# Weights split in place, identity products ahead of the first convolution, the rates moved behind the ring fills, and a last step without a recurrent state

## The chip, the cores and the metric

The kernel runs on one core of one Trainium2 chip. The metric is the device time of one execution in microseconds (us), as the median of several runs. The profile is of one execution; its span goes from the first to the last instruction.

## The reference, cut to what matters

Two layers are added onto `x` (128 batch rows, 128 time steps, 512 features), one after the other:

```python
# layer 0, a gated scan steered by cond (128 x 512)
conv = conv_b + causal convolution of x with cond as its 128 taps, per feature
proj = conv @ Wp + bp                      # 512 -> 128
B_t, C_t = softplus(proj[:64]), tanh(proj[64:])
u = x @ Ws + bs                            # 512 -> 64
dt = softplus(dt_log); decay = 1 - dt * softplus(A_log)
state = decay * state + dt * B_t * u ;  y = C_t * state
x = x + y @ Wo + bo
# layer 1, a recurrence over time, h0 = cond
h = tanh(h @ Wh + x[:, t] @ Wx + b)        # 512 -> 512
x[:, t] = x[:, t] + h
```

`dt` and `decay` (the "rates") come from two small vectors. `dt` is multiplied into the rows of `Wo`.

## The kernel before, in words

**Number format.** Most products are made with float32 operands split into a high part `*_hi` (type fp32r) and a rest `*_lo`. A weight is split by GpSimd (POOL): a cast to `*_hi`, then a subtraction into `*_lo`. The small weight Ws is split the same way into the two halves of `ws_hl`.

**Stage 1, four times (chunks c = 0 to 3 of 128 features).** `convolution(c)` (L713) makes 128 products of 128x128, one per feature; each shows as two PE records. Each 8 features are one slot of a ring of 8: `t_ring` (256 KB, the taps as a band) and `x_ring` (512 KB). SyncE (SP) loads a slot again once its 8 products are done (`load_next`, L235). VectorE (DVE) copies one half of a slot's band into place (`fill_band`, L527) before PE may use it; before that, eight memsets (L509) clear the ring's zero part. Four products fill a PSUM bank; ScalarE (ACT) copies the even banks to `conv` (L372), DVE the odd ones (L533). Then `split_projection(c)` (L735) turns the 32 blocks of `conv` (32 times 4 transposes, L753), ACT and DVE make the split `turned_hi` and `turned_lo`, and PE multiplies by Wp (L761 to L763). It starts when both copies of `conv` are complete and `wp_split` says that POOL has split this chunk's part of Wp.

**Ahead of chunk 0**, DVE's program is: the memsets, a wait for the small vectors, the rates (L511 to L524, two of the steps on ACT, L367 and L369), among them two multiplications that scale Wo (L520, L522), then `fill_band(0, 0)` (L575) and a wait until POOL has split Wo (L296, L298; it counts `weights_ready` to 1). POOL splits Wo first and Wp of chunk 0 next (`split_wp(0)`, L300). The loads of the vectors and of Wo stand in SP's queue behind those of ring slot 1.

**The last projection (chunk 3).** `last_projection()` (L828) is a plain float32 product: for each block m, PE turns block m (L845) and multiplies block n = m - 3 (L852, two records). ACT copies each turned block (L402), DVE adds each product to `bc` (L546, `last_add`). Products go through 4 banks: product n needs the adds up to n - 4. Between these adds DVE has the first softplus work: `soft_abs` (L589, four times, after m = 2 and 4) and `soft_sum` (L596, four times, after m = 6 and 7); between its copies ACT has the exponential and the logarithm (L432, L436, after m = 7 and 8) and a table load after m = 12. At m = 27 PE waits for `weights_ready` 4 and makes the first `u = x @ Ws`.

**Weights, during that projection.** SP issues Wx into a scratch tile `w_f`, x of group 0, b, h0 and Ws; waits for `weights_ready` 2; issues Wh into the same `w_f`; waits for the four soft sums (`b_ready` 4) and `weights_ready` 4; then loads x of group 1. POOL splits Wx (L317, L319), Wh (L321, L323), Ws (L325, L327), casts h0 and x (L332, L335), and makes the rests of both (L337, L343). `x_hi` has the place of `w_f`.

**The recurrence, 128 steps in 32 groups of 4.** `steps()` (L865 on PE) adds for each step the products of x and of h into one bank; DVE adds b (L679), ACT takes tanh (L483), PE transposes h (L875, 4 transposes), ACT casts it to `hT_hi` (L487), DVE makes `hT_lo` (L689) and adds h to x (L692). The next group's layer 0 is threaded between these. The last group stores each step by itself (L281, 256 KB).

Of the kernel before, what the change touches and what calls it, by code (L numbers as in the profile page):

```python
# [8 lines left out]
ALU = mybir.AluOpType  # L9
# [3 lines left out]
TIME = 128  # L13
# [13 lines left out]
LAG = 3  # L27
ODD = BANKS // 2 - 2
# [9 lines left out]
def build(nc, x_rev, x_dtb, bands, h0_t, vectors, Wp, Ws, Wo, Wx, Wh, b, out):  # L38
# [6 lines left out]
    with ctx:  # L45
# [46 lines left out]
        wx_hi = sb(ctx, "wx_hi", [P, KC, D], F32R)  # L92
        wx_lo = sb(ctx, "wx_lo", [P, KC, D], F32R)
        wh_hi = sb(ctx, "wh_hi", [P, KC, D], F32R)
        wh_lo = sb(ctx, "wh_lo", [P, KC, D], F32R)
        with ExitStack() as splitting:
            w_f = sb(splitting, "w_f", [P, KC, D])
# [4 lines left out]
        h0_f = sb(ctx, "h0_f", [P, KC, BATCH])  # L102
        ws_hl = sb(ctx, "ws_hl", [P, KC, 2 * N], F32R)
# [18 lines left out]
        ws_f = x_f[:, 1, EARLY].rearrange("p t b -> p (t b)")[:, 0:KC * N].rearrange("p (c n) -> p c n", c=KC)  # L122
# [93 lines left out]
        def _(sp):  # L216
# [37 lines left out]
            sp.dma_start(w_f[:], Wx.rearrange("(c p) n -> p c n", p=P)).then_inc(wx_loaded, DMA)  # L254
# [5 lines left out]
            load_x(0, 0)  # L260
            sp.dma_start(b_rows[:], b.partition_broadcast(P)).then_inc(late_loaded, DMA)
            sp.dma_start(h0_f[:], h0_t.rearrange("(c p) b -> p c b", p=P)).then_inc(late_loaded, DMA)

            sp.dma_start(ws_f, Ws.rearrange("(c p) n -> p c n", p=P)).then_inc(ws_loaded, DMA)
            sp.wait_ge(weights_ready, 2)
            sp.dma_start(w_f[:], Wh.rearrange("(c p) n -> p c n", p=P)).then_inc(wh_loaded, DMA)

            sp.wait_ge(b_ready, 2 * EARLY)
            sp.wait_ge(weights_ready, 4)
            load_x(1, 1)  # L270

            def stores_and_loads(g, par, first, last, j):
                if not (last or (isinstance(g, int) and g == GROUPS - 2)):

                    sp.wait_ge(x1_ready, KC * (g + 1))
                    load_x(g + 2, par)

                for s in range(0, G, 1 if last else G):
                    n = 1 if last else G
                    sp.wait_ge(out_ready, G * g + s + n)  # L280
                    sp.dma_start(out[:, bass.ds(g * G + s, n), :].rearrange("(c p) t b -> p c t b", p=P),  # L281
                                 x1_f[:, par, :, s:s + n]).then_inc(stored[par], DMA)
# [3 lines left out]
            sp.wait_ge(stored[1], DMA * (GROUPS // 2 - 1 + G))  # L286

        @block.gpsimd
        def _(pool):
# [18 lines left out]
            for c in range(1, KC - 1):  # L308
# [6 lines left out]
            pool.wait_ge(conv_done, BANKS * KC)  # L315
            pool.wait_ge(wx_loaded, DMA)
            nc.gpsimd.tensor_copy(wx_hi[:], w_f[:]).then_inc(pool_step, 1)  # L317
            pool.wait_ge(pool_step, 2)
            nc.gpsimd.tensor_tensor(wx_lo[:], w_f[:], f(wx_hi[:]), ALU.subtract).then_inc(weights_ready, 1)  # L319
            pool.wait_ge(wh_loaded, DMA)  # L320
            nc.gpsimd.tensor_copy(wh_hi[:], w_f[:]).then_inc(pool_step, 1)  # L321
            pool.wait_ge(pool_step, 3)
            nc.gpsimd.tensor_tensor(wh_lo[:], w_f[:], f(wh_hi[:]), ALU.subtract).then_inc(weights_ready, 1)  # L323
            pool.wait_ge(ws_loaded, DMA)
            nc.gpsimd.tensor_copy(ws_hl[:, :, 0:N], ws_f).then_inc(pool_step, 1)  # L325
            pool.wait_ge(pool_step, 4)
            nc.gpsimd.tensor_tensor(ws_hl[:, :, N:2 * N], ws_f, f(ws_hl[:, :, 0:N]), ALU.subtract)\  # L327
              .then_inc(weights_ready, 1)


            pool.wait_ge(late_loaded, 2 * DMA)
            nc.gpsimd.tensor_copy(hT_hi[:], h0_f[:]).then_inc(hthi_ready, 1)  # L332
            pool.wait_ge(weights_ready, 3)
            pool.wait_ge(x_loaded[0], DMA)
            nc.gpsimd.tensor_copy(x_hi[:], x_f[:, 0]).then_inc(xhi_ready, 1)  # L335
            pool.wait_ge(hthi_ready, 1)
            nc.gpsimd.tensor_tensor(hT_lo[:], h0_f[:], f(hT_hi[:]), ALU.subtract).then_inc(htlo_ready, 1)  # L337
# [14 lines left out]
            x_rest(0, 0)  # L352
            pool.wait_ge(ylo_ready, 1)
# [9 lines left out]
        def _(act):  # L363

            nc.scalar.preload_act_table_set("natural_log_exp_and_others")
            act.wait_ge(rate_step, 1)
            nc.scalar.activation(rates_e[:], rates[:, 0:2], ACT.Exp).then_inc(rate_act, 1)  # L367
            act.wait_ge(rate_act, 1)
            nc.scalar.activation(rates[:, 2:4], rates_e[:], ACT.Ln, bias=1.0).then_inc(rate_act, 1)  # L369

# [34 lines left out]
            copy_conv(0)  # L405
# [54 lines left out]
            for m in range(BANKS):  # L460
                copy_turned(KC - 1, m - m % 4, m % 4)
                if m in (7, 8):
                    soft_exp(m - 7, soft[m - 7])
                    soft_ln(m - 7, soft[m - 7])
                if m == 12:
                    nc.scalar.preload_act_table_set("exp_and_others")
                if m == 25:
                    tanh_c(0, 0)
                if m == 26:
                    u_copy(0)  # L470
                if m in (28, 29):
                    split_x_chunk(m - 28)
                if m == 30:
                    y_copy(0)
# [4 lines left out]
            def steps(g, par, first, last, j):  # L479
                for s in range(G):  # L480
# [3 lines left out]
                    if s == 2 and not last:  # L484
                        y_copy(g + 1)
                    act.wait_ge(ht_done, t + 1)
# [20 lines left out]
        def _(dve):  # L507
            for slot in range(RING):
                nc.vector.memset(t_ring[0:N, slot, 0], 0.0).then_inc(t_zero, 1)  # L509
            dve.wait_ge(vec_loaded, DMA)  # L510
            nc.vector.scalar_tensor_tensor(out=rates[:, 0:2], in0=logs, scalar=-1.0, in1=logs, op0=ALU.mult, op1=ALU.min)\  # L511
              .then_inc(rate_step, 1)
            dve.wait_ge(rate_act, 2)
            nc.vector.scalar_tensor_tensor(out=rates_e[:], in0=logs, scalar=0.0, in1=rates[:, 2:4], op0=ALU.max, op1=ALU.add)\
              .then_inc(rate_step, 1)
            dve.wait_ge(rate_step, 2)

            nc.vector.tensor_tensor(rates[:, 0:1], rates_e[:, 0:1], rates_e[:, 1:2], ALU.mult).then_inc(rate_step, 1)
            dve.wait_ge(wo_loaded, DMA)
            nc.vector.tensor_scalar(wo_f[N:P, :], wo_f[0:N, :], rates_e[0:N, 1:2], None, ALU.mult).then_inc(wo_scaled, 1)  # L520
            dve.wait_ge(wo_scaled, 1)
            nc.vector.tensor_scalar(wo_f[0:N, :], wo_f[0:N, :], rates_e[0:N, 1:2], None, ALU.mult).then_inc(wo_scaled, 1)  # L522
            dve.wait_ge(rate_step, 3)
            nc.vector.tensor_scalar(rates[:, 1:2], rates[:, 0:1], -1.0, 1.0, ALU.mult, ALU.add).then_inc(rate_step, 1)  # L524
# [7 lines left out]

            def copy_conv(c):  # L533
# [42 lines left out]
            dve.wait_ge(weights_ready, 1)  # L576
# [97 lines left out]
            def steps(g, par, first, last, j):  # L674
                for s in range(G):
# [9 lines left out]
                    if s == 1 and takes_sum(g, par):  # L685
                        for half in range(2):
                            soft_sum(j + EARLY - 1, g + 2 * EARLY - 2 + half, half, soft_f)
                    dve.wait_ge(hthi_ready, t + 2)
# [21 lines left out]
        def _(pe):  # L710
            pe.wait_ge(ident_ready, 1)

# [115 lines left out]
            def last_projection():  # L828
# [26 lines left out]

            last_projection()
            wo_product(0)
            z_recur(0, 0, start=True, stop=False)
# [6 lines left out]
            def steps(g, par, first, last, j):  # L865
                for s in range(G):
# [7 lines left out]
                    for k in range(KC):  # L874
                        mm = nc.tensor.transpose(HB[s % 2][:, bass.ts(k, P)], h_f[:, bass.ts(k, P)], ident[:])  # L875
# [62 lines left out]
```

## Time and profile before

| | us |
|---|---|
| median of 3 runs (lowest, highest) | 1181.25 (1179.35, 1182.19) |
| the profiled execution's own time | 1180.59 |
| its span | 1178.7 |
| PE busy | 1149.1 |
| DVE busy | 717.1 |
| ACT busy | 556.3 |
| POOL busy | 364.0 |

A row of the timeline gives start, duration, engine, line, operation, what it writes and reads, how often, and in brackets the idle time of that engine before it with what ended it. PE is busy for 97% of the span. It is idle for the other 29.6 us.

### The profile page before, as it was taken

Reading aid. Unit: us, or ns where it says so; the run is one execution under the profiler, and the core shown is the slowest. Engines: PE = TensorE matmul, PEld = TensorE weight load, DVE = VectorE, ACT = ScalarE, POOL = GpSimd, SP = SyncE. Lnnn points to the kernel's source line nnn. Section 1 sums busy time; section 2 is a strip of 40 time slices with the busy share of each in tenths; the row PEclk is TensorE's granted clock in tenths of the full one; section 3 lists DMA queues with packets and bytes.
Section 4 is the critical chain, followed back from the end, with each engine's and each line's share of the span. In section 5 each row is a group of like instructions: output and inputs, shape, how many; then the busy total and the mean of one; then the engine's idle time right before and its main releaser. Section 6 shows DMA issues by size and latency. Waiting matters only on the chain.

```text
span 1178.7 us, 16600 instructions
## 1 busy us (share of the span) xinstructions
PE 1149.1 (97%) x5984; PEld 953.7 (81%) x5984; DVE 717.1 (61%) x1158; ACT 556.3 (47%) x815; POOL 364.0 (31%) x210
## 2 busy tenths in 40 slices
PE   6999999988999999999999999999999999999997
PEld 6889898965788888888888888888888888888886
DVE  5786868776655555556555565555555655556553
ACT  2574737454345445453545454544545354545431
POOL 1000504134133333333333333333333333333330
PEclk9999999999999999999999999999999999999999
DMA  9719092631122222222222222222222222222202
GB/s 357 294 55 378 3 340 94 217 132 36 37 72 72 72 82 94 87 92 72 71 71 71 71 71 71 71 71 82 94 85 94 72 71 71 71 71 72 72 36 72
DMA packets 56899, 121.35 MB, mean 103 GB/s; under 512 B 3936, under 2 KB 7008, under 8 KB 56864
## 3 DMA queue, kind: packets, MB, share of 16 engines
q1 hardware_dynamic: 56864, 120.87, 30.3%
q8 instruction: 24, 0.39, 0.1%
q14 instruction: 11, 0.09, 0.0%
HBM read 87.30 MB, written 33.55 MB: 103 GB/s over the span
## 4 chain that ended last, share of the span: by engine, by line
PE 95%; DVE 2%; issue 1%; DMA 0%; ACT 0%; POOL 0%; SPq 0%; POOLq 0%; DVEq 0%; ACTq 0%
PE bank L813 10%; PE bank L731 10%; PE bank L821 10%; PE bank L822 10%; PE bank L807 10%; PE bank L825 10%; PE bank L806 10%; PE bank L875 5%; PE bank L753 3%; PE bank L780 3%; PE bank L786 3%; PE bank L796 2%; PE bank L797 2%; PE bank L761 2%; PE bank L762 2%; PE bank L763 2%
## 5 line engine op out<-in xcount | busy, mean ns | idle before, releaser
L349 POOL TENSOR_TENSOR x_lo<-x_f,x_hi 128x512 fp32r<-128x512 f32 x124 | 156.6, 1293 | 555.9 <-ACT x_hi L451 555.9
L483 ACT ACTIVATE h_f<-z_f 128x512 f32<-128x512 f32 x128 | 80.9, 632 | 295.0 <-DVE z_f L679 295.0
L689 DVE TENSOR_TENSOR hT_lo<-bank,hT_hi 128x512 fp32r<-128x512 f32 x128 | 88.6, 692 | 187.7 <-ACT hT_hi L487 187.7
L821 PE MATMUL bank<-wh_hi,hT_hi 128*128 128x512 f32 x512 | 200.4, 391 | 0.0
L822 PE MATMUL bank<-wh_lo,hT_hi 128*128 128x512 f32 x512 | 199.9, 390 | 0.0
L807 PE MATMUL bank<-wx_lo,x_hi 128*128 128x512 f32 x512 | 199.6, 390 | 0.0
L806 PE MATMUL bank<-wx_hi,x_hi 128*128 128x512 f32 x512 | 199.2, 389 | 0.0
L679 DVE TENSOR_TENSOR z_f<-bank,b_rows 128x512 f32<-128x512 f32 x128 | 88.6, 692 | 130.0 <-PE bank L825 129.3
L343 POOL TENSOR_TENSOR x_lo<-x_f,x_hi 128x2048 fp32r<-128x2048 f32 x32 | 147.7, 4615 | 18.3 <-ACT x_hi L456 18.3
L813 PE MATMUL bank<-wx_hi,x_lo 128*128 128x512 f32 x512 | 144.8, 404 | 0.3 <-POOL x_lo L349 0.3
L825 PE MATMUL bank<-wh_hi,hT_lo 128*128 128x512 f32 x512 | 137.1, 389 | 0.0
L731 PE MATMUL bank<-t_ring,x_ring 128*128 128x128 f32 x1024 | 117.7, 279 | 11.8 <-DVE t_ring L531 11.6
L731 PEld LDWEIGHTS bank<-t_ring,x_ring 128*128 128x128 f32 x1024 | 117.3, 195 | 12.7 <-issue 11.6
L487 ACT CAST hT_hi<-bank 128x512 fp32r<-128x512 f32 x128 | 75.2, 587 | 95.5 <-PE bank L875 95.5
L821 PEld LDWEIGHTS bank<-wh_hi,hT_hi 128*128 128x128 f32 x512 | 96.1, 188 | 26.0 <-ACT hT_hi L487 6.1
L451 ACT CAST x_hi<-x_f 128x512 fp32r<-128x512 f32 x128 | 79.6, 622 | 76.9 <-DVE x_f L639 74.6
L825 PEld LDWEIGHTS bank<-wh_hi,hT_lo 128*128 128x128 f32 x512 | 96.1, 188 | 20.4
L807 PEld LDWEIGHTS bank<-wx_lo,x_hi 128*128 128x128 f32 x512 | 96.1, 188 | 20.0
L806 PEld LDWEIGHTS bank<-wx_hi,x_hi 128*128 128x128 f32 x512 | 96.1, 188 | 19.9
L822 PEld LDWEIGHTS bank<-wh_lo,hT_hi 128*128 128x128 f32 x512 | 96.2, 188 | 19.5
L813 PEld LDWEIGHTS bank<-wx_hi,x_lo 128*128 128x128 f32 x512 | 91.2, 188 | 17.3 <-POOL x_lo L349 0.6
L639 DVE SCALAR_TENSOR_TENSOR x_f<-bank,vec,x_f 128x512 f32<-128x512 f32 x128 | 90.0, 745 | 4.8 <-PE bank L797 4.1
(89 smaller groups left out, 1631.6 us busy)
## 6 DMA issues: line engine op xcount, KB each, us to landing
x_ring<-x_rev SPq DMA_DIRECT2D x64, 512.0 KB, 7.6
x_f<-x_dtb SPq DMA_DIRECT2D x32, 1024.0 KB, 8.4
out<-x_f SPq DMA_DIRECT2D x31, 1024.0 KB, 5.3
t_ring<-bands SPq DMA_DIRECT2D x64, 256.0 KB, 6.7
w_f<-Wx SPq DMA_DIRECT2D x1, 1024.0 KB, 5.4
w_f<-Wh SPq DMA_DIRECT2D x1, 1024.0 KB, 5.1
out<-x_f SPq DMA_DIRECT2D x4, 256.0 KB, 2.3
turned<-Wp SPq DMA_DIRECT2D x3, 128.5 KB, 3.0
```

The lines of the kernel that those rows point to most:

```text
L343: nc.gpsimd.tensor_tensor(x_lo[:], x_f[:, par], f(x_hi[:]), ALU.subtract).then_inc(xlo_ready, 1)
L349: nc.gpsimd.tensor_tensor(x1_lo[:, c], x1_f[:, par, c], f(x1_hi[:, c]), ALU.subtract)\
L639: nc.vector.scalar_tensor_tensor(out=x1_f[:, par, c].rearrange("p t b -> p (t b)"), in0=XB[c][:], scalar=bo_c[:, c:c + 1], in1=x_f[:, par, ...
L679: nc.vector.tensor_tensor(z_f[:], ZB[s % 2][:], b_rows[:], ALU.add).then_inc(zsum_ready, 1)
L689: nc.vector.tensor_tensor(hT_lo[:], turned_h, f(hT_hi[:]), ALU.subtract).then_inc(htlo_ready, 1)
L731: mm = nc.tensor.matmul(to, x_ring[:, slot, d % CH], t_ring[:, slot, :, d % CH], start=True, stop=True)
L806: nc.tensor.matmul(z, x1_hi[:, k, s], wx_hi[:, k], start=start and k == 0, stop=False)
L807: nc.tensor.matmul(z, x1_hi[:, k, s], wx_lo[:, k], start=False, stop=False)
L813: mm = nc.tensor.matmul(z, x1_lo[:, k, s], wx_hi[:, k], start=False, stop=stop and k == KC - 1)
L821: nc.tensor.matmul(z, hT_hi[:, k], wh_hi[:, k], start=start and k == 0, stop=False)
L822: nc.tensor.matmul(z, hT_hi[:, k], wh_lo[:, k], start=False, stop=False)
L825: mm = nc.tensor.matmul(z, hT_lo[:, k], wh_hi[:, k], start=False, stop=stop and k == KC - 1)
```

## The change

1. PE: after the identity is there, 11 products identity times identity into a bank not yet in use.
2. The loads of the vectors and of Wo move behind those of ring slot 7. DVE's rates move from ahead of `fill_band(0, 0)` into `copy_conv(0)`, behind the fill of slot 15 and ahead of the copy of bank 29; ACT's two steps go behind its copy of bank 28. POOL still splits Wo ahead of Wp of chunk 0. DVE's wait for `weights_ready` 1 stands behind the copies of chunk 0.
3. `wx_f` and `wh_f` have the places of `wx_lo` and `wh_lo`, `ws_f` that of `ws_hl`: POOL subtracts in place. `w_f` is gone, and SP issues Ws, Wx, x of group 0, Wh, h0 and b with no wait between them. x of group 1 waits for `b_ready` 4 and for the first turned block.
4. POOL's order is Ws, Wx, (wait for `b_ready` 4) cast of x, rest of x, Wh, h0. `weights_ready` 2 now means Ws, 3 Wx, 4 Wh. PE's wait at m = 27 is for 2, and one for 4 stands ahead of the first recurrent product.
5. DVE's soft work: `soft_abs` after m = 4, 5, 6, 7, each behind a wait for `weights_ready` 3; `soft_sum` after m = 8 to 11. ACT: exponentials after m = 9 and 11, logarithms after 10 and 12, the table load after 14.
6. The last step makes no `hT_hi` and `hT_lo`; its transposes go to two banks, two each, and DVE's add and SP's store are done in two halves.

```diff
@@ memory
         wx_hi = sb(ctx, "wx_hi", [P, KC, D], F32R)
+        with ExitStack() as splitting:
+            wx_f = sb(splitting, "wx_f", [P, KC, D])
         wx_lo = sb(ctx, "wx_lo", [P, KC, D], F32R)
...
-        with ExitStack() as splitting:
-            w_f = sb(splitting, "w_f", [P, KC, D])
...
+            ws_f = sb(splitting, "ws_f", [P, KC, 2 * N])
         ws_hl = sb(ctx, "ws_hl", [P, KC, 2 * N], F32R)
@@ sync
-                if n == 1:
+                if n == RING - 1:
                     sp.dma_start(vec[:], vectors).then_inc(vec_loaded, DMA)
                     sp.dma_start(wo_f[0:N, :], Wo).then_inc(wo_loaded, DMA)
...
             sp.wait_ge(conv_done, BANKS * KC)
-            sp.dma_start(w_f[:], Wx...).then_inc(wx_loaded, DMA)
+            sp.dma_start(ws_f[:, :, N:], Ws...).then_inc(ws_loaded, DMA)
+            sp.dma_start(wx_f[:], Wx...).then_inc(wx_loaded, DMA)
             load_x(0, 0)
+            sp.dma_start(wh_f[:], Wh...).then_inc(wh_loaded, DMA)
+            sp.dma_start(h0_f[:], h0_t...).then_inc(late_loaded, DMA)
             sp.dma_start(b_rows[:], b.partition_broadcast(P)).then_inc(late_loaded, DMA)
-            sp.dma_start(h0_f[:], h0_t...).then_inc(late_loaded, DMA)
-            sp.dma_start(ws_f, Ws...).then_inc(ws_loaded, DMA)
-            sp.wait_ge(weights_ready, 2)
-            sp.dma_start(w_f[:], Wh...).then_inc(wh_loaded, DMA)
             sp.wait_ge(b_ready, 2 * EARLY)
-            sp.wait_ge(weights_ready, 4)
+            sp.wait_ge(turn_done, BANKS * (KC - 1) + 1)
             load_x(1, 1)
@@ gpsimd
-            pool.wait_ge(conv_done, BANKS * KC)
+            pool.wait_ge(ws_loaded, DMA)
+            nc.gpsimd.tensor_copy(ws_hl[:, :, 0:N], ws_f[:, :, N:]).then_inc(pool_step, 1)
+            pool.wait_ge(pool_step, 2)
+            nc.gpsimd.tensor_tensor(ws_hl[:, :, N:], ws_f[:, :, N:], f(ws_hl[:, :, 0:N]), ALU.subtract)\
+              .then_inc(weights_ready, 1)
             pool.wait_ge(wx_loaded, DMA)
+            nc.gpsimd.tensor_copy(wx_hi[:], wx_f[:]).then_inc(pool_step, 1)
             pool.wait_ge(pool_step, 3)
+            nc.gpsimd.tensor_tensor(wx_lo[:], wx_f[:], f(wx_hi[:]), ALU.subtract).then_inc(weights_ready, 1)
+            pool.wait_ge(b_ready, 2 * EARLY)
             pool.wait_ge(x_loaded[0], DMA)
             nc.gpsimd.tensor_copy(x_hi[:], x_f[:, 0]).then_inc(xhi_ready, 1)
             pool.wait_ge(turn_done, BANKS * (KC - 1) + 5)
...
             x_rest(0, 0)
+            pool.wait_ge(wh_loaded, DMA)
+            nc.gpsimd.tensor_copy(wh_hi[:], wh_f[:]).then_inc(pool_step, 1)
+            pool.wait_ge(pool_step, 4)
+            nc.gpsimd.tensor_tensor(wh_lo[:], wh_f[:], f(wh_hi[:]), ALU.subtract).then_inc(weights_ready, 1)
+            pool.wait_ge(late_loaded, 2 * DMA)
+            nc.gpsimd.tensor_copy(hT_hi[:], h0_f[:]).then_inc(hthi_ready, 1)
@@ scalar
-            act.wait_ge(rate_step, 1)
-            nc.scalar.activation(rates_e[:], rates[:, 0:2], ACT.Exp).then_inc(rate_act, 1)
...
+            for m in range(0, BANKS, 2):
+                act.wait_ge(conv_done, m + 1)
+                nc.scalar.copy(conv[:, :, bass.ts(m, PER_BANK)], ...).then_inc(conv_copied_act, 1)
+                if m == BANKS - 4:
+                    act.wait_ge(rate_step, 1)
+                    nc.scalar.activation(rates_e[:], rates[:, 0:2], ACT.Exp).then_inc(rate_act, 1)
...
-                if m in (7, 8):
-                    soft_exp(m - 7, soft[m - 7])
-                    soft_ln(m - 7, soft[m - 7])
-                if m == 12:
+                if m in (9, 11):
+                    soft_exp((m - 9) // 2, soft[(m - 9) // 2])
+                if m in (10, 12):
+                    soft_ln((m - 10) // 2, soft[(m - 10) // 2])
+                if m == 14:
@@ vector
+                    if c == 0 and n == P // CH - 2:
+                        rates_of_state()
...
+                if c == 0:
+                    dve.wait_ge(weights_ready, 1)
...
-                if m in (2, 4):
-                    q = m // 2 - 1
-                    dve.wait_ge(proj_added, m)
-                    for n in (2 * q, 2 * q + 1):
-                        soft_abs(n, n % 2, soft[q])
-                if m in (6, 7):
-                    for par in range(2):
-                        soft_sum(m - 6, 2 * (m - 6) + par, par, soft[m - 6])
+                if m in (4, 5, 6, 7):
+                    n = m - 4
+                    dve.wait_ge(weights_ready, 3)
+                    dve.wait_ge(proj_added, n + 1)
+                    soft_abs(n, n % 2, soft[n // 2])
+                if m in (8, 9, 10, 11):
+                    n = m - 8
+                    soft_sum(n // 2, n, n % 2, soft[n // 2])
...
+                    if last and s == G - 1:
+                        for half in (slice(0, KC // 2), slice(KC // 2, KC)):
+                            dve.wait_ge(ht_done, TIME + (half.start > 0))
+                            turned_half = HB[int(half.start > 0)][:].rearrange("p (c b) -> p c b", c=KC)[:, half]
+                            nc.vector.tensor_tensor(x1_f[:, par, half, s, :], turned_half, x1_f[:, par, half, s, :],
+                                                    ALU.add).then_inc(out_ready, 1)
+                        continue
@@ tensor
             pe.wait_ge(ident_ready, 1)
+            for _ in range(IDLE):
+                nc.tensor.matmul(bank[7][:, 0:P], ident[:], ident[:], start=True, stop=True)
...
-                        pe.wait_ge(weights_ready, 4)
+                        pe.wait_ge(weights_ready, 2)
```

## Rows read from the trace of the kernel before

**Rows 1.** The page, its first part: busy us (share of the span) and instructions
```profile
PE 1149.1 (97%) x5984; PEld 953.7 (81%) x5984; DVE 717.1 (61%) x1158; ACT 556.3 (47%) x815; POOL 364.0 (31%) x210
```

**Rows 2.** Timeline of all engines, 0 to 45 us
```profile
0.91 4.27 DVE L509 MEMSET t_ring<- 64x512 f32 x8 [0.91 <-PEq L929]
1.19 0.29 POOL L292 TENSOR_SCALAR_AFFINE_SELECT ident<-ident 128x128 f32<-128x128 f32 x1 [0.24 <-POOL ident L290]
...
8.58 0.20 ACT L367 ACTIVATE rates_e<-rates 128x2 f32<-128x2 f32 x1 [6.55 <-DVE rates L511]
...
10.49 0.61 POOL L296 CAST wo_hi<-turned 128x512 fp32r<-128x512 f32 x1 [9.01 <-DVE turned L522]
10.52 0.86 DVE L531 COPY t_ring<-t_ring 64x512 f32<-64x512 f32 x1
11.19 1.32 POOL L298 TENSOR_TENSOR wo_lo<-turned,wo_hi 128x512 fp32r<-128x512 f32 x1
...
11.64 31.35 PE L731 MATMUL bank<-t_ring,x_ring 128*128 128x128 f32 x256 [11.64 <-DVE t_ring L531]
...
20.89 0.40 POOL L302 CAST wp_hi<-turned 128x256 fp32r<-128x256 f32 x1 [8.38 <-DMA turned<-Wp]
...
21.37 0.73 POOL L305 TENSOR_TENSOR wp_lo<-turned,wp_hi 128x256 fp32r<-128x256 f32 x1
...
27.63 0.33 SPq L225 DMA_DIRECT2D x_ring<-x_rev  x1
...
43.82 1.39 PE L753 MATMUL bank<-ident,conv 128*128 128x128 f32 x11 [0.83 <-issue]
```

**Rows 3.** PE's line L731 alone, 11.6 to 16 us: ns of a record, min/median/max
```profile
L731 PE MATMUL bank<-t_ring,x_ring x20: 421/421/553, 11.6 to 15.8; 128*128 128x128 f32 x20
```

**Rows 4.** Windows, line L731: PE busy (records), PEld, PEclk, DMA share, GB/s
```profile
17.00:42.00 25.00, 25.00 (x226) 25.00 (x226) 1.00 1.04 400
```

**Rows 5.** Transfers issued between 27.6 and 28.2 us (slot 14): size, us from issue to landing
```profile
x_ring<-x_rev SPq DMA_DIRECT2D x1, 512.0 KB, 8.4
```

**Rows 6.** Timeline of all engines, 240 to 292 us
```profile
245.72 0.69 SPq L264 DMA_DIRECT2D x_f<-Ws  x1
...
246.09 1.02 PE L852 MATMUL bank<-turned,wp_now 128*128 128x512 f32 x2
...
249.09 1.90 POOL L317 CAST wx_hi<-w_f 128x2048 fp32r<-128x2048 f32 x1 [35.71 <-DMA w_f<-Wx]
...
251.06 4.58 POOL L319 TENSOR_TENSOR wx_lo<-w_f,wx_hi 128x2048 fp32r<-128x2048 f32 x1
...
255.96 0.63 ACT L432 ACTIVATE x_f<-x_f 128x512 f32<-128x512 f32 x1 [3.79 <-DVE x_f L589]
...
257.16 0.86 DVE L589 TENSOR_SCALAR x_f<-bc 64x512 uint32<-64x512 uint32 x2
...
261.30 6.84 DVE L596 SCALAR_TENSOR_TENSOR bc<-bc,x_f 64x512 f32<-64x512 f32 x2
...
268.16 3.10 DVE L546 TENSOR_TENSOR bc<-bank,bc 128x512 f32<-128x512 f32 x5
...
269.00 1.53 PE L852 MATMUL bank<-turned,wp_now 128*128 128x512 f32 x2 [4.86 <-DVE bc L546]
...
273.36 1.02 PE L852 MATMUL bank<-turned,wp_now 128*128 128x512 f32 x2
...
285.03 1.02 PE L852 MATMUL bank<-turned,wp_now 128*128 128x512 f32 x2
```

**Rows 7.** Windows, PE alone: busy (records), PEclk, DMA share, GB/s
```profile
269.00:273.40 4.40, 4.40 (x13) 0.61 0.67 195
```

**Rows 8.** Timeline of all engines, 1173 us to the end
```profile
1173.33 0.66 PE L875 MATMUL bank<-ident,h_f 128*128 128x128 f32 x4 [1.45 <-ACT h_f L483]
...
1175.25 0.68 DVE L692 TENSOR_TENSOR x_f<-bank,x_f 128x512 f32<-128x512 f32 x1
1175.96 0.37 SPq L281 DMA_DIRECT2D out<-x_f  x1
```

More of the change, by code:

```diff
@@ L27 @@
 LAG = 3
+IDLE = 11
 ODD = BANKS // 2 - 2
@@ L102, in build @@
         h0_f = sb(ctx, "h0_f", [P, KC, BATCH])
+        with ExitStack() as splitting:
+            ws_f = sb(splitting, "ws_f", [P, KC, 2 * N])
         ws_hl = sb(ctx, "ws_hl", [P, KC, 2 * N], F32R)
@@ L279, in stores_and_loads @@
                     n = 1 if last else G
+                    if last and s == G - 1:
+                        for half in (slice(0, KC // 2), slice(KC // 2, KC)):
+                            sp.wait_ge(out_ready, TIME + (half.start > 0))
+                            sp.dma_start(out[half.start * P:half.stop * P, TIME - 1:, :]
+                                         .rearrange("(c p) t b -> p c t b", p=P),
+                                         x1_f[:, par, half, s:]).then_inc(stored[par], DMA)
+                        continue
                     sp.wait_ge(out_ready, G * g + s + n)
@@ L352, in _ @@
             x_rest(0, 0)
+            pool.wait_ge(wh_loaded, DMA)
[4 more added lines that the diff above has]
+            nc.gpsimd.tensor_copy(hT_hi[:], h0_f[:]).then_inc(hthi_ready, 1)
+            pool.wait_ge(hthi_ready, 1)
+            nc.gpsimd.tensor_tensor(hT_lo[:], h0_f[:], f(hT_hi[:]), ALU.subtract).then_inc(htlo_ready, 1)
             pool.wait_ge(ylo_ready, 1)
@@ L403, in copy_turned @@
                   .then_inc(turn_copied, 1)
-            copy_conv(0)
+            for m in range(0, BANKS, 2):
+                act.wait_ge(conv_done, m + 1)
+                nc.scalar.copy(conv[:, :, bass.ts(m, PER_BANK)],
+                               CONV[m % 4][:].rearrange("p (d l) -> p l d", d=PER_BANK)).then_inc(conv_copied_act, 1)
+                if m == BANKS - 4:
+                    act.wait_ge(rate_step, 1)
+                    nc.scalar.activation(rates_e[:], rates[:, 0:2], ACT.Exp).then_inc(rate_act, 1)
+                    act.wait_ge(rate_act, 1)
+                    nc.scalar.activation(rates[:, 2:4], rates_e[:], ACT.Ln, bias=1.0).then_inc(rate_act, 1)
             act.wait_ge(vec_loaded, DMA)
@@ L485, in steps @@
                         y_copy(g + 1)
+                    if last and s == G - 1:
+                        continue
                     act.wait_ge(ht_done, t + 1)
@@ L509, in _ @@
                 nc.vector.memset(t_ring[0:N, slot, 0], 0.0).then_inc(t_zero, 1)
[L510 to L524, printed above, removed]
             decay = rates[N:P, 1:2]
@@ L575, in _ @@
             fill_band(0, 0)
-            dve.wait_ge(weights_ready, 1)
             chunk(0)
@@ L687, in steps @@
                             soft_sum(j + EARLY - 1, g + 2 * EARLY - 2 + half, half, soft_f)
+                    if last and s == G - 1:
+                        for half in (slice(0, KC // 2), slice(KC // 2, KC)):
+                            dve.wait_ge(ht_done, TIME + (half.start > 0))
+                            turned_half = HB[int(half.start > 0)][:].rearrange("p (c b) -> p c b", c=KC)[:, half]
+                            nc.vector.tensor_tensor(x1_f[:, par, half, s, :], turned_half, x1_f[:, par, half, s, :],
+                                                    ALU.add).then_inc(out_ready, 1)
+                        continue
                     dve.wait_ge(hthi_ready, t + 2)
@@ L854, in last_projection, with turned_to @@
                 pe.wait_ge(proj_added, added_before + 29)
+            def turned_to(s, k, end):
+                to = HB[0] if end and k < KC // 2 else HB[s % 2]
+                return to[:, bass.ts(k, P)]
             last_projection()
             wo_product(0)
+            pe.wait_ge(weights_ready, 4)
             z_recur(0, 0, start=True, stop=False)
@@ L874, in steps @@
                     for k in range(KC):
-                        mm = nc.tensor.transpose(HB[s % 2][:, bass.ts(k, P)], h_f[:, bass.ts(k, P)], ident[:])
+                        if end and k == KC // 2:
+                            mm.then_inc(ht_done, 1)
+                        mm = nc.tensor.transpose(turned_to(s, k, end), h_f[:, bass.ts(k, P)], ident[:])
                     mm.then_inc(ht_done, 1)
```

46 lines of the change are left out of this document (22 added, 24 removed).

## The prediction, made before the changed kernel ran

> **What bounds the kernel now.** The page first: PE is busy for 1149.1 of 1178.7 us [rows 1], so the change can gain where PE idles or runs slowly, and nowhere else. The timeline shows three such places. Ahead of the first convolution PE waits until 11.64 us, for the fill of slot 0 at 10.52, which stands behind the rates and the scaling of Wo in DVE's program, though the eight memsets end at 5.2 us [rows 2]. In the last projection PE's block pace is 1.297 us (nine blocks, n = 14 to 23, from 273.36 to 285.03), but from block 0 at 246.09 to block 14 it takes 27.27 us, where 14 x 1.297 = 18.16 would do: 9.1 us are lost [rows 6]. The cause is DVE. A soft_abs takes 0.43 us (two in 0.86) where POOL rests, and two soft sums take 6.84 us, 5 us more than two others, while POOL runs a subtraction; with one soft_abs that stood for 4.6 us beside POOL's 4.58 us, DVE is stopped twice and the adds behind it come late [rows 6]. PE idles 4.86 us at the second stop, and its granted clock is then 0.61 in the mean of 4.4 us, so for part of them the lower level, 1.2 GHz [rows 6, 7]. Third, the end: the last add, 1175.25 to 1175.93, stands behind hT_hi and hT_lo, which nobody reads [rows 8]. The recurrence between is not touched.
>
> **Part 1, the start.** PE's 11 products are 22 records. At the pace of the first records (421 ns long, 20 starting in 4.2 us, so 0.22 apart) [rows 3] they take 4.8 us from 1.5 us, when the identity is there [rows 2], to 6.3. DVE fills slot 0 after the memsets at 5.2, for 0.4. So the convolution begins at 6.3 rather than 11.64. But it doesn't end 5.3 earlier. At full clock PE needs 25.0/226 x 16 = 1.77 us for a slot, while a slot's 786 KB take 1.96 us at the 400 GB/s at which the transfer engines run without a gap [rows 4]. Before, PE hid this behind its late start. An earlier reload request only waits longer in a full queue, and moving 130 KB from slot 2 to slot 8 changes nothing for slot 14. So slot 14 is there when it was, at 27.63 + 8.4 = 36.0 us [rows 2, 5], slot 15 1.96 later, and the convolution ends at 38.0 + 1.8 = 39.8 against 43.0 before.
>
> Then a new chain decides. ACT's exponential waits for the copy of bank 28, the first half of slot 14: 36.0 + 0.9 + 0.1 + 0.65 (an ACT pass over 512 columns, 0.63 [rows 6]) = 37.7. From the exponential (8.58) to POOL's first cast (10.49) were 1.9 us; POOL's Wo part takes 11.19 + 1.32 - 10.49 = 2.0, its Wp part 21.37 + 0.73 - 20.89 = 1.2 [rows 2]. With 0.15 for handovers, Wp is split at 37.7 + 1.9 + 2.0 + 1.2 + 0.15 = 42.95 and PE turns the first block at 43.05, not at 43.82. DVE's copies of banks 29 and 31 end at 41.2 and are covered by this; if the chain were gone they would let PE go at 41.3. One more term: DVE's fill of the next slot 0 comes at about 41.2, against POOL's Wo subtraction. The row of such a meeting shows DVE's fill stretched from 0.4 to 0.86 and POOL not delayed (L531 beside L296) [rows 2]; by it the gain is 0.8. I take 0.6, for a delay of POOL from nothing to the 0.4 of a fill. Bounds for this part: -1.2 (one late transfer of 1.8 us) and +2.6 (the chain hidden).
>
> The Trainium skill, SBUF — State Buffer, "SBUF: two separate sides", says that DVE in a two-port mode and GpSimd hold a shared port pair for a whole instruction, whichever comes first. By that rule POOL's Wp cast waits for the fill in turn and this part's gain would be 0.4, not 0.8.
>
> **Part 2, the last projection.** SP issues Ws first (0.69 us [rows 6]), so Wx starts 0.7 later, and Ws's 128 KB in 256-byte pieces take between 0.33 us (at 400 GB/s) and four times that. Wx is there at 249.0 + 0.9 = 249.9. POOL needs 1.90 + 0.1 + 4.58 [rows 6]: `weights_ready` is 3 at 256.5. DVE does adds 0 to 4 by 253.0 (block 4 begins at 251.3 and takes 1.0, its add 0.7), then idles at its wait; behind it are all further adds. Adds take 0.62 to 0.69 [rows 6], so add 5 ends at 256.5 + 0.45 + 0.7 = 257.65. PE needs it for block 9, due at 246.09 + 9 x 1.297 = 257.76: no stall. ACT's first exponential waits for the second soft_abs, 258.1, and its copy of block 10 ends at 258.1 + 0.65 + 0.7 = 259.45 where PE wants it at 259.06: a stall of 0.4. Each further pair of blocks gives ACT 2.59 us for two copies and two soft passes, 2.7 us, until block 12, then the table load; I add 0.3. No DVE soft operation now meets a POOL instruction, since POOL waits for `b_ready` 4, at about 266. So 0.7 us is lost instead of 9.1: a gain of 8.4, with bounds of 6.0 (Wx or POOL 2 us later) and 9.1 (no loss). The clock's cost is in this figure, for without an idle stretch the clock should stay.
>
> Is what was moved behind it in time? POOL casts x (1.90) and makes its rest (4.6) by 272.6; PE wants it at about 277. Wh takes 6.5 more, h0 2: 281.2; PE wants it at 299 - 8.4 = 291. x of group 1, asked for at 266 on an idle queue, lands near 272 (1 MB at 400 GB/s is 2.6 us, and as much again for the way) and is first read after 280. All three are covered by 4 us or more. SP's queue past the wait for `b_ready` holds only that load and the stores. u's product with B_t (two SBUF inputs) falls at about 281, where POOL may still be at h0: up to 0.7 us, in the bounds.
>
> **Part 3, the end.** The first two transposes end about 1173.7, the others 1173.99. A half add costs between 0.34 and 0.68 (half and whole of L692); I take 0.48: done at 1174.7, and the store is issued then, not at 1175.96 [rows 8]. The other store's 0.37 us of issue fits in between. Gain 1.2; bounds 0.8 and 1.5.
>
> **Sum.** 0.6 + 8.4 + 1.2 = 10.2 against the profiled execution's 1180.59: 1170.4. The median stands 0.66 above that execution, so I forecast 1171.0.
>
> **Rivals.** (a) *Clock.* PE now idles from 39.8 to 43.05, 3.2 us. After 4.86 us the clock fell, and blocks 12 and 13 took 273.36 - 269.00 = 4.36 for 2.59 [rows 6, 7]: 1.8 us. For it: the length is near; against: it is shorter. 1172.8. Beside this rule of the row the Trainium skill, TensorE: Matmul & The Clock Gate, "Part 1", says that idleness brings the lower clock and that the moment depends on a phase that the kernel doesn't set; by it some executions pay and others don't. (b) *The start gains nothing or loses*, because a transfer lags or the chain is longer: 1171.6 to 1173. (c) *The start isn't bound by transfers* and the chain begins 3.5 us sooner: 1167.3. Against it speaks the full queue [rows 4]. (d) *The wait of DVE in the last projection ends 3 to 5 us late*, for Wx or for a slower subtraction in place: each us after 256.6 costs one: 1174 to 1176, and the clock may fall with it. (e) *Slower than before.* The same place: DVE's wait for `weights_ready` 3 holds all adds. It decides once POOL's subtraction in place takes 4.6 + 10.2 - 1.8 = 13 us or more; at four times its price, 18.3 us, the sum is 1171.0 + 13.6 + 1.8 = 1186.4. For it only that no row shows POOL writing over its own source. (f) *The change doesn't do what it says*: the soft operations still meet POOL, as the order of waits would have to allow; the gain is then 2 to 4, 1178.
>
> **Chances.** Forecast 0.55; (a) 0.14; (b) 0.12; (c) 0.05; (d) 0.09; (e) 0.02; (f) 0.03. About 0.3% (3.5 us) is what a measurement can tell from no change. Faster by more: all but (e), and half of (f): 0.95; same 0.03; slower 0.02. The range takes in (a), (b), (c) and most of (d): 1167.3 to 1175.0.
>
> **What would show it.** The convolution's PE row beginning near 6.3 and lasting some 33 us, with small idle times that end with a transfer; PE idle for 3 us before L753 with POOL's Wp subtraction as its releaser; block 14 of L852 18.9 us after block 0, not 27.27; soft_abs at 0.43 and soft sums at 0.68 each; POOL's subtraction at 4.6 in place; the last store issued 0.7 us after the last transpose, not 2.0. I am wrong if soft operations still take 4 us, if PE idles over 2 us between 250 and 270, or if the first block is turned before 42 or after 45 us.

## The result, and the profile after

The changed kernel takes 1170.18 us in the median of 4 runs (1169.57 to 1170.76), the kernel before, with one more run, 1181.72 (1179.35 to 1182.41): a ratio of 0.9906 with a 95% interval of 0.9889 to 0.9923, so about 11 us or 0.9% less. The forecast was 1171.0, range 1167.3 to 1175.0. The profiled execution took 1170.19 us, with a span of 1168.4.

| stretch | before | after | gain | forecast |
|---|---|---|---|---|
| start to block 0 of the last projection | 246.09 | 246.32 | -0.2 | 0.6 |
| block 0 to block 14 | 27.27 | 18.46 | 8.8 | 8.4 |
| block 14 to the first add of b | 31.64 | 31.64 | 0.0 | 0 |
| recurrence, first add of b to last | 866.92 | 866.83 | 0.1 | 0 |
| last add of b to the end | 6.78 | 5.15 | 1.6 | 1.2 |
| span | 1178.7 | 1168.4 | 10.3 | 10.2 |

The sum is right to 0.1 us, its first term is not. The page's first line, to be read beside [rows 1], shows PE busier though 10 us are gone: its work is the same but for 22 records, and its idle time fell from 29.6 to 15.5 us.

```profile
PE 1152.9 (99%) x6006; PEld 957.3 (82%) x6006; DVE 707.0 (61%) x1158; ACT 555.6 (48%) x814; POOL 363.2 (31%) x210
```

**The start.** The timeline of the changed kernel, 0 to 50 us, beside [rows 2]:

```profile
1.54 4.41 PE L739 MATMUL bank<-ident 128*128 128x128 f32 x22 [1.54 <-POOL ident L301]
...
5.22 0.42 DVE L529 COPY t_ring<-t_ring 64x512 f32<-64x512 f32 x1
...
5.78 1.98 PE L759 MATMUL bank<-t_ring,x_ring 128*128 128x128 f32 x16
...
23.36 2.02 PE L759 MATMUL bank<-t_ring,x_ring 128*128 128x128 f32 x16 [0.84 <-DMA x_ring<-x_rev]
...
37.49 0.21 ACT L413 ACTIVATE rates_e<-rates 128x2 f32<-128x2 f32 x1
...
38.06 2.02 PE L759 MATMUL bank<-t_ring,x_ring 128*128 128x128 f32 x16 [0.20 <-DMA x_ring<-x_rev]
...
39.41 0.61 POOL L305 CAST wo_hi<-turned 128x512 fp32r<-128x512 f32 x1 [37.93 <-DVE turned L545]
...
42.00 0.72 POOL L314 TENSOR_TENSOR wp_lo<-turned,wp_hi 128x256 fp32r<-128x256 f32 x1
...
42.87 3.49 PE L781 MATMUL bank<-ident,conv 128*128 128x128 f32 x16 [2.78 <-POOL wp_lo L314]
```

The convolution starts at 5.78 and ends at 40.08; its idle times end with transfers, and slot 15 starts at 38.06, where the forecast had 38.0. The chain of rates, Wo and Wp then ends where it was worked out: PE turns the first block at 42.87 (forecast 43.05, before 43.82). But those 16 transposes take 3.49 us. Before, all 16 of them took 1.94. The windows of PE alone (us, busy with records, granted clock, transfer share, GB/s) say why:

```profile
40.00:42.80 2.80, 0.08 (x1) 0.97 1.04 402
42.80:46.10 3.30, 3.23 (x16) 0.51 1.03 399
46.10:50.00 3.90, 3.90 (x25) 1.00 1.04 402
```

The clock fell to 1.2 GHz behind an idle time of 2.8 us and was back at 46.1, when the first product of the projection began. That product, first before and then after the change:

```profile
46.18 0.50 PE L761 MATMUL bank<-turned_hi,wp_hi 128*128 128x512 f32 x1 [0.42 <-DVE turned_lo L552]
```

```profile
46.11 0.48 PE L789 MATMUL bank<-turned_hi,wp_hi 128*128 128x512 f32 x1
```

Before, PE had to wait 0.42 us for DVE's split here; now that wait lies under the slow transposes. So the transposes are 1.55 us longer, but the way from the first transpose to the first product is only 0.88 us longer (3.24 for 2.36), and it is 0.86 longer to the next block's first product. The fall costs 0.9 us, and of the head start of 0.95 only 0.07 is left.

The other 0.3 us of this stretch go in the convolution of chunk 2. PE's row of it, before and after, and two rows of the changed kernel inside it:

```profile
147.74 28.82 PE L731 MATMUL bank<-t_ring,x_ring 128*128 128x128 f32 x256
```

```profile
147.65 29.14 PE L759 MATMUL bank<-t_ring,x_ring 128*128 128x128 f32 x256
```

```profile
150.43 0.73 POOL L314 TENSOR_TENSOR wp_lo<-turned,wp_hi 128x256 fp32r<-128x256 f32 x1
150.43 1.00 DVE L529 COPY t_ring<-t_ring 64x512 f32<-64x512 f32 x1
```

Here DVE's fill meets POOL's split of Wp and takes 1.00 instead of 0.42. Before, the same subtraction began 0.94 us later and missed the fill. In e5, e8, e10 and e12 a fill of this chunk takes 0.87 to 0.97 us and the convolution 29.00 to 29.10; in e2 no fill is stretched, and it takes 28.82.

**The last projection**, beside [rows 6]:

```profile
246.32 1.02 PE L880 MATMUL bank<-turned,wp_now 128*128 128x512 f32 x2
...
252.16 4.53 POOL L332 TENSOR_TENSOR wx_lo<-wx_f,wx_hi 128x2048 fp32r<-128x2048 f32 x1
...
256.73 0.42 DVE L608 TENSOR_SCALAR x_f<-bc 64x512 uint32<-64x512 uint32 x1 [3.46 <-POOL wx_lo L332]
...
259.49 1.12 PE L880 MATMUL bank<-turned,wp_now 128*128 128x512 f32 x2
...
263.58 0.67 DVE L615 SCALAR_TENSOR_TENSOR bc<-bc,x_f 64x512 f32<-64x512 f32 x1
...
264.78 1.02 PE L880 MATMUL bank<-turned,wp_now 128*128 128x512 f32 x2
...
265.64 1.89 POOL L336 CAST x_hi<-x_f 128x2048 fp32r<-128x2048 f32 x1 [8.95 <-DVE bc L615]
```

Every soft operation now has its own price, 0.42 and 0.67 to 0.69, where the two that were stopped took 4.6 and 4.9. DVE waits 3.46 us for POOL, but with five adds done; POOL waits 8.95 us for DVE. The subtraction in place costs 4.53, as much as before. Block 10, at 259.49, is late by 0.2 us, for ACT's copy (the forecast had 0.4 there), and block 14 stands at 264.78.

**The end**, beside [rows 8]:

```profile
1164.65 0.66 PE L911 MATMUL bank<-ident,h_f 128*128 128x128 f32 x4 [1.44 <-ACT h_f L494]
1165.13 0.76 DVE L711 TENSOR_TENSOR x_f<-bank,x_f 128x256 f32<-128x256 f32 x2 [1.19 <-PE bank L911]
1165.58 0.89 SPq L285 DMA_DIRECT2D out<-x_f  x2
```

Each half add takes 0.42, both together 0.76 since they overlap, and they are over 0.58 us after the last transpose, not 1.94.

### The profile page after: what moved, and what is told of

The parts are those of the page before. It is cut to its first block, busy times and chain, and to the rows that moved or that the text cites. A ratio compares the mean times of both kernels' runs of the same rounds, so it can differ in the third digit from the quotient of the medians.

```text
span 1168.4 us, 16597 instructions
## 1 busy us (share of the span) xinstructions
PE 1152.9 (99%) x6006; PEld 957.3 (82%) x6006; DVE 707.0 (61%) x1158; ACT 555.6 (48%) x814; POOL 363.2 (31%) x210
## 4 chain that ended last, share of the span: by engine, by line
PE 96%; DMA 1%; SPq 1%; POOL 1%; issue 0%; DVE 0%; ACT 0%; POOLq 0%; DVEq 0%; ACTq 0%
PE bank L841 10%; PE bank L849 10%; PE bank L850 10%; PE bank L835 10%; PE bank L853 10%; PE bank L834 10%; PE bank L759 8%; PE bank L911 5%; PE bank L781 4%; PE bank L814 3%; PE bank L808 3%; PE bank L824 2%; PE bank L825 2%; PE bank L880 2%; PE bank L789 2%; PE bank L790 2%
## 6 DMA issues: line engine op xcount, KB each, us to landing
wh_f<-Wh SPq DMA_DIRECT2D x1, 1024.0 KB, 10.3
```

## The experiments

The account to be tested: (1) the gain of the last projection comes from keeping DVE's soft operations and POOL's two-input instructions apart; (2) the start gives nothing, because transfers, POOL's chain and the clock each take a part; (3) the end gives 1.6 us. The kernel before was measured again beside each group of four, on the same chip: 1180.47 (e1 to e4), 1181.23 (e5 to e8), 1181.4 (e9 to e12). Ratios are to it, with 95% intervals.

**e1, the end alone**, on the kernel before: the diff's parts in `stores_and_loads`, `steps` of ACT, DVE and PE.

> The kernel before with part 6 of the change alone (last step without hT_hi and hT_lo, add and store in halves). My account of the two traces puts 1.6 us on it: from the last add of b to the end 6.78 us before, 5.15 after. So 1180.1 us against 1181.7, and a last stretch of 5.1 to 5.2 us. Rival: the store's way to memory hides it, and the time stays within 0.3 us of before.

Measured: 1179.08, ratio 0.9988 (0.9979 to 0.9998). From the last add of b to the end 5.15 us. So the end is worth 1.4 us by the medians and 1.6 by the profiles, of its own; the interval alone would allow 0.2 to 2.5.

**e2, the start undone**, on the changed kernel:

```diff
-IDLE = 11
+IDLE = 0
-                if n == RING - 1:
+                if n == 1:
                     sp.dma_start(vec[:], vectors)
...
+            rates_of_state()
             fill_band(0, 0)
+            dve.wait_ge(weights_ready, 1)
             chunk(0)
```

> The changed kernel with parts 1 and 2 undone (no identity products, rates and Wo scaling ahead of the first fill, vectors and Wo loaded behind slot 1). Theory: the start brings nothing on balance, since the convolution is held by the transfers until 40.1 us, POOL's splits until 42.9, and the clock then falls and takes the rest. So 1169.7 to 1170.7 us, first block turned at 43.8 us at full clock, block 0 of the last projection at 246.1. Rival: the earlier start is worth its 0.6 us or more without the fall, which was chance, and this kernel is slower than the changed one by 0.6 to 2 us.

Measured: 1169.8, ratio 0.9912 (0.9895 to 0.9928): the same as the changed kernel. No fall of the clock: first block at 43.48, all 16 transposes in 1.94, block 0 of the last projection at 245.74. Parts 1 and 2 of the change bring nothing as they stand.

**e3, the rates four slots earlier**, on the changed kernel; and **e12**, the same kernel again:

```diff
-                    if c == 0 and n == P // CH - 2:
+                    if c == 0 and n == 10:
                         rates_of_state()
...
-                if m == BANKS - 4:
+                if m == 20:
                     act.wait_ge(rate_step, 1)
```

> The changed kernel with the rates four slots earlier (DVE behind the fill of slot 11, ACT behind its copy of bank 20), so that Wo and Wp are split before the convolution ends. Theory: the chain of rates, Wo and Wp holds PE from 41.2 to 42.87 us and makes the idle stretch long enough for the clock to fall. Here the first block is turned at 41.2, behind DVE's copy of bank 31, PE idles 1.1 us, the clock stays: 1.7 + 1.5 = 3.2 us less, 1167.0. Rival: the transfers or the copies hold PE anyway, and less than 0.5 us is gained.

> The kernel of e3 once more, on the chip of the others of this call, since e5 and e3 were on chips that differ by 0.8 us for the kernel before. Theory: a ratio to before of 0.9875 to 0.989; executions with a mean clock of 1.0 are 13.5 to 14.5 us below before, and each fall of the clock, in a wait for transfers, costs 1.5 to 3 us.

Measured: e3 1166.99, ratio 0.9884 (0.9868 to 0.9901), e12 1168.45, ratio 0.9888 (0.9872 to 0.9905). The two medians differ by 1.5 us, of which 0.9 is between the kernels before. All four executions of e12 have a mean clock of 1.0 and lie 12.7 to 13.3 us below the kernel before, not the 13.5 to 14.5 that I expected. The profiled execution of e12 shows the mechanism that was expected, no fall of the clock and no wait for POOL:

```profile
33.18 7.38 PE L759 MATMUL bank<-t_ring,x_ring 128*128 128x128 f32 x64 [0.75 <-DVE t_ring L529]
41.40 1.94 PE L781 MATMUL bank<-ident,conv 128*128 128x128 f32 x16 [0.83 <-issue]
```

The first row also shows a price that I had left out: the rates hold DVE, the fill of slot 12 comes late, and the convolution ends at 40.56. The profiled execution of e3 (1169.41, the slowest of its four; the others 1166.0 to 1167.5) went otherwise. PE waited 2.34 us for slot 8, and the windows of PE alone show what followed:

```profile
23.00:25.50 2.50, 0.17 (x2) 0.94 1.01 392
25.50:29.40 3.90, 3.88 (x21) 0.60 1.03 399
```

Its first block was turned at 43.48. So a wait for transfers can drop the clock too.

**e4, POOL isn't held**, on the changed kernel:

```diff
-            pool.wait_ge(b_ready, 2 * EARLY)
             pool.wait_ge(x_loaded[0], DMA)
```

> The changed kernel without POOL's wait for b_ready 4, so that POOL goes on with x, Wh and h0 beside DVE's soft operations. Theory: what the change gains in the last projection it gains by keeping POOL's two-input instructions away from those operations; here they meet again, single soft operations last 2 to 5 us, PE idles 5 us or more with a fall of the clock: 1175 to 1179. Rival: the later places of the soft operations and the loads without waits gain it, the wait is of no account, and the time stays at 1170.

Measured: 1180.85, ratio 1.0003 (0.9993 to 1.0012), more than the 1175 to 1179 expected. One line takes back all 11 us. Block 14 comes 29.5 us after block 0, later than before the change (27.3). The timeline, then PE's windows:

```profile
257.03 2.08 DVE L607 TENSOR_SCALAR x_f<-bc 64x512 uint32<-64x512 uint32 x1 [3.42 <-POOL wx_lo L332]
...
258.98 4.50 POOL L341 TENSOR_TENSOR x_lo<-x_f,x_hi 128x2048 fp32r<-128x2048 f32 x1
...
259.73 4.03 DVE L607 TENSOR_SCALAR x_f<-bc 64x512 uint32<-64x512 uint32 x1
...
265.05 1.65 PE L879 MATMUL bank<-turned,wp_now 128*128 128x512 f32 x2 [3.67 <-ACT turned L403]
```

```profile
257.00:276.00 19.00, 11.85 (x37) 0.82 0.00 1
```

The second soft_abs ends with POOL's instruction (263.76, after 258.98 + 4.50 = 263.48) and not 0.42 after its own start.

**e5, 30 identity products**, on e3; **e11, 20 of them**, on e3:

```diff
-IDLE = 11
+IDLE = 30
```

> The kernel of e3 with 30 identity products instead of 11. They end near 10.8 us, so the convolution begins 5 us later, and by its full pace (28.3 us) would end at 39.1; the transfers let it end at about 40.1. Theory: nothing is lost by the later start, since only the transfers count, and PE waits 1 us in the convolution rather than 6, so that the clock has no cause to fall there, as it did in e3's profiled execution (2.3 us of waiting for slot 8, then 0.72 of the clock, first block at 43.5 instead of 41.2). All executions then lie at 1166.0 to 1166.8 with a mean clock of 0.999 or 1, where e3's spread over 3.4 us. Rival: the transfers aren't the limit, the later start comes out at the end, and this kernel is slower than e3 by 2 us or more.

> The kernel of e3 with 20 identity products, ending near 8.6 us: between e3 (11, convolution from 5.8) and e5 (30, from 11.05, convolution's end at 40.9). Theory: the transfers hold the end at 40.1 still, the first block is turned at 41.2, and the waits for transfers are too short for the clock to fall in most executions. The ratio to before is 0.9875 to 0.988, with a spread under 1.5 us. Rival: the same 0.9884 as e3 and e5.

Measured: e5 1167.9, ratio 0.9888 (0.9872 to 0.9905), its four runs within 0.8 us; e11 1168.05, ratio 0.9884 (0.9867 to 0.99), within 2.2 us. In e5 the convolution starts at 11.05 and ends at 40.94, in e12, which has 11 products and no other difference, at 6.19 and 40.56: 4.9 us of head start are worth 0.4 at its end. So the transfers are the limit. But neither kernel is better than e3: e5 missed the 1166.0 to 1166.8 expected, and the ratio foretold for e11 was not reached, 0.9884 is its rival's. The narrower spread of e5 agrees with a clock that never falls there; four runs don't show more.

**e6 and e10, identity products in the gap** before the first block, on the changed kernel. In e6 they stand behind PE's waits for the copies of conv, in e10 ahead of them:

```diff
             for c in range(KC - 1):
                 convolution(c)
+                if c == 0:
+                    for _ in range(10):
+                        nc.tensor.matmul(bank[7][:, 0:P], ident[:], ident[:], start=True, stop=True)
                 released = split_projection(c)
```

> The changed kernel with 10 more identity products between the first convolution and the wait for the splits (20 records, 2.2 to 2.5 us of the gap of 2.8). Theory: PE turns the first block at 42.9 as in the changed kernel, but at full clock, and saves the 1.5 us that the fall costs: 1168.7. Rival: the fall in that gap was chance in the profiled execution, and the median stays at 1170.2 within 0.5.

> The changed kernel with 10 identity products right behind the first convolution, ahead of PE's wait for the copies of conv (in e6 they stood behind it and ran on until 45.0 us, past POOL's splits). They run from 40.1 to 42.5 us. Theory: the first block is turned at 42.9 at full clock in executions where the clock fell in that gap, 1.5 us less: 0.9 to 1.5 us below the changed kernel's ratio to before, so a ratio of 0.9895. Rival: the clock falls in the waits for transfers instead, and the ratio stays at 0.9906.

Measured: e6 1170.75, ratio 0.9911 (0.9895 to 0.9928); e10 1170.05, ratio 0.9901 (0.9885 to 0.9918). e6 was a test badly made. Its products began only at 42.71, behind DVE's copies, and ran until 45.0, past POOL's last subtraction. Its profiled execution is also disturbed earlier: PE waits 2.47 us for slot 8, the clock is 0.53 from 25.4 to 29.0, and the convolution ends at 41.6.

```profile
42.71 2.47 PE L779 MATMUL bank<-ident 128*128 128x128 f32 x20 [1.10 <-DVE conv L557]
...
43.96 0.72 POOL L314 TENSOR_TENSOR wp_lo<-turned,wp_hi 128x256 fp32r<-128x256 f32 x1
...
45.02 1.25 PE L784 MATMUL bank<-ident,conv 128*128 128x128 f32 x10
```

In e10 they are in place and the clock holds (16 transposes in 1.94), but in that execution PE's slots 7 to 9 began 1.0 to 1.2 us later than in the changed kernel, long before the added products. POOL's chain came 1.2 us later too, and the block was turned at 44.09:

```profile
40.87 2.40 PE L799 MATMUL bank<-ident 128*128 128x128 f32 x20
44.09 1.94 PE L781 MATMUL bank<-ident,conv 128*128 128x128 f32 x16 [0.83 <-POOL wp_lo L314]
```

Its ratio is 0.6 us better than that of the changed kernel, within both intervals. Both expectations took the fall at 1.5 us, the length by which the transposes grow, where the path grows by 0.9. A gain of 0.9 can't be told from none with these intervals: the two runs neither confirm nor refute that the median pays it.

**e7, no identity products**, on the changed kernel (`IDLE = 0`).

> The changed kernel without its 11 identity products. Theory: they bring nothing, since the first slots run at the lower clock into waits for transfers; the convolution still ends at 40.0 to 40.2 and the time is 1170.2 within 0.5. Rival: they raise the clock before real work, which is worth the 2 us that the slow records cost before: 1172.

Measured: 1170.62, ratio 0.9913 (0.9896 to 0.993): no difference. PE's convolution line up to 8 us (ns of a record, min/median/max), first in e7, then in the changed kernel:

```profile
L759 PE MATMUL bank<-t_ring,x_ring x10: 421/421/553, 5.9 to 7.9; 128*128 128x128 f32 x10
```

```profile
L759 PE MATMUL bank<-t_ring,x_ring x16: 275/275/307, 5.8 to 7.5; 128*128 128x128 f32 x16
```

The products do bring the clock up before real work. It is worth nothing there: both convolutions end at 40.1, at the pace of the transfers.

**e8, the soft operations at their old places**, on the changed kernel: DVE's loops around the soft operations put back as they were, without the wait for `weights_ready` 3.

> The changed kernel with DVE's and ACT's soft operations back at their old places (after m = 2, 4, 6, 7 and 7, 8) and no wait for weights_ready 3. Theory: what counts is that POOL rests until b_ready 4. The first two soft_abs pass before POOL's subtraction of Wx, the second pair is stopped by it until 256.7 us, which is the time until which DVE waits in the changed kernel anyway; so 1170.2 within 0.7, one soft_abs of 3 to 4 us, PE idle for less than 1.5 us. Rival: the new places and the wait are what gains, and this loses 4 us or more.

Measured: 1174.05, ratio 0.994 (0.9923 to 0.9956), 4 us slower than the changed kernel by the ratios; block 14 comes 22.1 us after block 0, where it was 18.5. My expectation was wrong, and so was its picture of the first pair:

```profile
250.15 1.89 POOL L330 CAST wx_hi<-wx_f 128x2048 fp32r<-128x2048 f32 x1 [2.48 <-DMA wx_f<-Wx]
...
250.87 6.11 DVE L607 TENSOR_SCALAR x_f<-bc 64x512 uint32<-64x512 uint32 x2
...
252.12 4.57 POOL L332 TENSOR_TENSOR wx_lo<-wx_f,wx_hi 128x2048 fp32r<-128x2048 f32 x1
...
257.84 1.19 PE L879 MATMUL bank<-turned,wp_now 128*128 128x512 f32 x2 [1.99 <-DVE bc L563]
```

POOL's cast already meets it. DVE is stopped until 256.98, about as long as the changed kernel's DVE waits (256.73), but with three adds done instead of five, and PE's ring of four banks runs dry at block 7. The clock then falls (0.51 from 258.8 to 262.2 us). The late places are worth their two adds.

**e9, the hold alone**, on the kernel before:

```diff
+            pool.wait_ge(b_ready, 2 * EARLY)
             pool.wait_ge(wh_loaded, DMA)
             nc.gpsimd.tensor_copy(wh_hi[:], w_f[:]).then_inc(pool_step, 1)
```

> The kernel before with one line added: POOL waits for b_ready 4 ahead of the split of Wh. Theory: of the 9.1 us lost in the last projection the larger part is the second stop of DVE (the soft sums beside the split of Wh, PE idle 4.86 us and the fall of the clock behind it); the first stop (soft_abs beside the split of Wx) remains. So block 14 begins 20 to 22 us after block 0 instead of 27.3, and the time is 5 to 7 us below before: 1175. POOL's later work (Ws, h0, x) then ends near 279 us, where PE wants it at about 280, so a wait of up to 1 us can appear at m = 27. Rival: the loads without waits and the new places are needed, POOL's work comes too late at m = 27, and less than 2 us is gained.

Measured: 1174.23, ratio 0.9938 (0.9921 to 0.9954), 7.2 us below before. Block 14 comes 20.5 us after block 0. The first stop stays, the second is gone, and POOL still is in time for m = 27:

```profile
250.63 5.60 DVE L590 TENSOR_SCALAR x_f<-bc 64x512 uint32<-64x512 uint32 x2
...
259.56 1.40 DVE L597 SCALAR_TENSOR_TENSOR bc<-bc,x_f 64x512 f32<-64x512 f32 x2
...
263.06 1.90 POOL L322 CAST wh_hi<-w_f 128x2048 fp32r<-128x2048 f32 x1 [7.11 <-DVE bc L597]
```

Of the 8.8 us of the last projection the hold gives 27.3 - 20.5 = 6.8 without any split in place; the other 2.0 are the first stop.

## Why the prediction was right, and where not

**Part 2, the last projection: right.** Its reading of the two stops, what removes them, the time of `weights_ready` 3 (256.5, found 256.7), add 5 just in time and ACT's copy of block 10 as the one stall all stand in the trace; the gain was 8.8 for 8.4, since block 10 was late by 0.2 and not 0.4 and ACT's later passes cost 0.1 and not 0.3. That the stops are POOL's doing, which the trace before only suggested, e4 and e9 show from both sides. This bears out what the Trainium skill says in SBUF — State Buffer, "SBUF: two separate sides": a DVE operation in a two-port mode or with two inputs in SBUF and a GpSimd instruction do not share, one blocks for the whole length of the other. In e4 a soft_abs of 0.42 stands for 4.03 us and ends 0.28 us after POOL's subtraction; that soft_abs, with its one input, runs in such a mode is not shown by any run. DVE's adds, which have one input in PSUM, keep their 0.69 us beside the same instructions. Rival (e), a dear subtraction in place, is out: 4.53 us.

**Part 1, the start: the term is off by 0.8 us (-0.2 for 0.6), and the step that failed is the one after the chain.** The transfers as the limit, slots 14 and 15 at the times worked out, the chain of 6.9 us and its end (42.87 for 43.05) are confirmed, and e5 (beside e12) and e7 show independently that neither an earlier start nor a warm clock reaches the end of the convolution. POOL wasn't delayed by the fill at 40.84 beyond 0.2 us (its cast took 0.59 where [rows 2] has 0.40), which is between the two values that were weighed. So the first block gained 0.95 us. But rival (a) came true in the profiled execution: the clock fell behind 2.8 us of idleness. It took 0.9 and not the rival's 1.8, because here half of it lies over a wait that was there anyway. I had given it 0.14, since the idle time worked out, 3.2 us, is shorter than 4.86. That was a weak argument, with one fall and no shorter stretch to compare. The last 0.3 was in no term: a fill of chunk 2 that met POOL. It is the meeting that the change removes from the last projection, and where it falls hangs on when Wp lands.

**Part 3, the end: right in kind, 0.4 too small.** The adds are over 0.58 us after the last transpose, where the forecast had 0.7. The other 0.3 was in no term: a half store lands 1.9 us after its issue, the whole one took 2.3, and from the end of the last add to the end of the kernel are 2.5 us, not 2.8. e1 shows this part by itself.

**The sum** was right to 0.1 us because these errors cancel: 0.8 too much at the start, 0.4 and 0.4 too little after it. That is luck. The 0.66 us that the forecast added for the median didn't come back: the profiled execution of the changed kernel lies at its median, 0.8 us under the forecast. **The chances**: the forecast case is what happened in two of three parts, with rival (a) on top, inside the range.

What stays open: how often the clock falls in the changed kernel. Four profiled executions have its start and nothing in the gap: the changed kernel, e4, e7 and e8. PE idles 2.78 to 3.06 us in all four, the clock falls in all four, and the 16 transposes take 3.1 to 3.6 us. The mean clocks of the other executions agree with a fall in most, but not surely in all: 0.997 to 0.999 in the changed kernel, 0.999 to 1 in e2 and e10. What the fall is worth in the median, e6 and e10 were to single out and didn't. That the kernels with the earlier rates are about 2 us faster is surer: the intervals of the ratios overlap, but all 16 executions of e3, e5, e11 and e12 (1166.0 to 1169.41) lie at or below the 20 of the changed kernel, e2, e6, e7 and e10 (1169.41 to 1171.88).

## What to carry to other kernels

Look for DVE operations with long times beside POOL instructions, and before moving work or memory try one wait that keeps POOL out of that stretch: here one line gave 7 of 11 us. A head start of an engine is worth only what the next resource lets through; set the transfer pace of a slot beside the compute pace before counting it. And when a serial chain (rates, Wo, Wp) is moved off the front, put it where it ends before it is wanted: four slots earlier gave about 2 us that the change itself left behind.

## What the runs showed of the hardware that was not expected

The clock fell behind idle times of PE of 2.8 us (changed kernel), 2.5 us (e6), 2.3 us (e3) and 2.0 us (e8, ahead of 257.84), not only behind 4.9, and stayed through idle times of 1.8 us (e11, before 25.2) and 1.5 us (before, ahead of block 7). The same kernel can go either way: e3's profiled execution had a fall in the convolution, behind a wait of 2.3 us, and e12's had none, its longest wait there being 1.0 us.

A fall of the clock costs less than the slow records show where a wait of another engine would have stood behind them: 1.55 us of longer transposes were 0.9 us of time.

Single transfers of a ring that is loaded without a gap can come late while the rate stays near 400 GB/s. In the changed kernel PE waits 0.6 to 0.8 us for slots 7 to 9 and under 0.3 for all others; for slot 8 alone it waits 2.3 us in e3, 2.5 in e6 and 1.8 in e11. Why is not shown.

And a POOL cast, with one input, stops a soft_abs just as a subtraction does: in e4 the one at 257.03 takes 2.08 us beside a cast of 1.90 that began at 256.93, and e8's first pair meets one too.
